# A decoder layer with routed experts on one core: routing, shared expert and experts joined into one stage

## The reference

```
x = layernorm(x + self_attention(x))            # 16 heads of 16, rotary
x = layernorm(x + cross_attention(x, ctx_1024)) # one head of 256
x = layernorm(x + ffn(x))

# ffn, over N = 4096 rows of D = 256
shared = silu(x @ sg.T) * (x @ su.T) @ sd.T     # hidden width 704, padded to 768
shared = shared * sigmoid(x @ shared_gate_w.T)
probs = softmax(x @ gate_w.T)                   # 16 experts
rw, sel = top_k(probs, 2);  rw = rw / rw.sum()
g, h = split(x @ w_gate_up[e]);  expert_e = silu(g) * h @ w_down[e]
ffn = sum over the two chosen e of rw_e * expert_e + shared
```

## Time and profile before

| | |
|---|---|
| three runs | 1185.35, 1186.81 (median), 1187.66 us |
| the profiled execution | 1185.7 us, with a span of 1183.9 us inside it |
| TensorE (PE) busy | 874.0 us, 74% |
| VectorE (DVE) busy | 724.5 us, 61% |
| ScalarE (ACT) busy | 435.5 us, 37% |
| GpSimd (POOL) busy | 409.4 us, 35% |
| mean granted TensorE clock | 0.884 of 2.4 GHz |

### The profile page before, as it was taken

How to read it: one execution, slowest core, us unless ns; L and a number is a source line. 1 busy time by engine, 2 the same in 40 slices (tenths; PEclk the granted TensorE clock), 3 DMA queues, 4 the chain that set the end, 5 groups by cost and what they waited for, 6 DMA issues and landing times. The chain is left out here.

```text
span 1183.9 us, 20916 instructions
## 1 busy us (share of the span) xinstructions
PE 874.0 (74%) x6264; PEld 706.6 (60%) x6265; DVE 724.5 (61%) x1546; ACT 435.5 (37%) x968; POOL 409.4 (35%) x500
## 2 busy tenths in 40 slices
PE   3588888888877288888888410999678778789492
PEld 2465555555544277778777300888578668777382
DVE  5467777767773267777777395244255556467575
ACT  2036565656667133333333122222134334321120
POOL 4322323232310133333333172666500000177664
PEclk8679999999999599999999555899888899999797
DMA  1969989998982724444443344333333344234222
GB/s 62 238 154 248 210 240 219 230 223 209 237 202 60 148 47 99 106 101 106 95 103 80 101 132 150 126 126 107 120 116 116 112 127 135 83 103 143 87 86 71
DMA packets 193065, 161.47 MB, mean 136 GB/s; under 512 B 82160, under 2 KB 179056, under 8 KB 189936
## 3 DMA queue, kind: packets, MB, share of 16 engines
q1 hardware_dynamic: 176368, 133.45, 44.4%
q0 software_dynamic: 6144, 16.79, 4.4%
q10 hardware_dynamic: 10496, 10.49, 2.8%
HBM read 80.86 MB, written 75.37 MB: 132 GB/s over the span
## 5 line engine op out<-in xcount | busy, mean ns | idle before, releaser
L543 DVE TENSOR_REDUCE neg_m<-ps_s 128x2 f32<-128x512 f32 x256 | 169.1, 688 | 37.1 <-PE ps_s L303 36.8
L106 PE MATMUL ps_f<-xg,w_sgu 128*128 128x512 f32 x576 | 146.7, 405 | 48.9 <-DMA xg<-x2T_parts 48.0
L437 ACT ACTIVATE probs<-ps_t 128x512 f32<-128x512 f32 x256 | 147.1, 598 | 95.6 <-PE ps_t L309 91.2
L303 PE MATMUL ps_s<-k_stack,q_stack 48*128 48x256 f32 x512 | 119.0, 335 | 52.6 <-DVE neg_m L543 42.4
L106 PEld LDWEIGHTS ps_f<-xg,w_sgu 128*128 128x128 f32 x576 | 108.8, 195 | 74.0 <-DMA xg<-x2T_parts 49.2
L303 PEld LDWEIGHTS ps_s<-k_stack,q_stack 48*128 48x128 f32 x512 | 76.3, 195 | 109.0 <-DVE neg_m L543 57.0
L309 PE MATMUL ps_t<-q_stack,k_stack 49*128 49x256 f32 x512 | 117.2, 328 | 2.7 <-ACT probs L437 2.7
L106 PE MATMUL ps_g<-w_qkv,x_hl 128*128 128x512 f32 (+1 forms) x384 | 90.9, 386 | 18.6 <-DVE w_qkv L469 11.2
L1426 PE MATMUL ps_f<-w_sdn,hid_hl 128*128 128x256 f32 x576 | 81.8, 294 | 28.3 <-DVE hid_hl L1547 27.9
L1426 PEld LDWEIGHTS ps_f<-w_sdn,hid_hl 128*128 128x128 f32 x576 | 77.5, 198 | 36.5 <-DVE hid_hl L1547 32.3
L106 PE MATMUL ps_f<-w_gu,hid_hl 128*128 x474 | 85.6, 322 | 2.3 <-issue 1.7
(11 more groups left out here) (182 smaller groups left out, 1771.5 us busy)
## 6 DMA issues: line engine op xcount, KB each, us to landing
stacks<-q_hl SPq DMA_DIRECT2D x48, 256.0 KB, 2.8
stacks<-k_hl SPq DMA_DIRECT2D x48, 256.0 KB, 3.5
q_stack<-stacks SPq DMA_DIRECT2D x32, 384.0 KB, 5.8
k_stack<-stacks SPq DMA_DIRECT2D x32, 384.0 KB, 9.2
expert_rows<-no_rows ACTq DMA_DIRECT2D x16, 640.0 KB, 5.5
rows<-expert_rows SPq DMA_DIRECT2D x79, 128.0 KB, 2.1
expert_outputs<-rows SPq DMA_DIRECT2D x79, 128.0 KB, 1.7
heads_out<-o_sb SPq DMA_DIRECT2D x32, 256.0 KB, 9.8
```

Source lines behind the costliest of these rows:

```text
L106: last = pe.matmul(out, lhs(l, c), rhs(r, c), start=(n == 0), stop=(n == len(todo) - 1))
L303: by_query = pe.matmul(ps_s[n % 2][:, k * N:(k + 1) * N], q[q_rows, slab, k * P:(k + 1) * P], kk[q_rows, slab, :], start=True, stop=True)
L437: act.activation(probs[:, n % RING], ps_t[n % 2].rearrange("p (t q) -> p t q", t=TT), ACT.Exp).then_inc(exp_done, 1)
L543: dve.tensor_reduce(neg_m[c][:, :, row], ps_s[n % 2].rearrange("p (t k) -> p t k", t=TT), AX.X, ALU.max, negate=True).then_inc(max_done, 1)
```

## The change

- `routing` and `feed_forward` become one stage, `back_end`. The shared expert starts at once; its first 30 chunks (`EARLY` = 5 groups) run before the experts, 18 after.
- The shared expert's weights are loaded and split in `self_attention`, one piece of 512 columns in each of nine steps: loaded by SP, copied by ACT, subtracted by POOL.
- The routing chain of DVE is cut into pieces that stand between the chunks 0 to 8. PE's two products stand before chunk 4 and use the banks of that chunk.
- The experts' weights are split between the chunks 10 to 21, two pieces of 512 columns in each, by ACT and DVE. POOL splits nothing there.
- POOL's two copies for a tile are gone: the indirect transfers read `pos` and the tile where they lie. As `outputs` overwrites the tile, it waits for the tile's scatter; for the first two groups the result is held in a buffer (`hold`) and added later (`add_held`).
- `BY` is 16, and the check of the loaded values' bounds is left out.
- After the experts the gathered rows have 32 buffers (the dead `w_gu`) in place of 4. POOL takes the root for two tiles at once, and DVE combines two tiles at once; it does 13 of the 16 pairs between the 18 chunks. All of this is written out without loops.

```diff
@@ self_attention, SP, at the end of step(i)
+                j = i.n - S_FIRST
+                if 0 <= j < S_PIECES:
+                    if j >= 2:
+                        sp.wait_ge(s_lo, j - 1)
+                    raw = s_raw[j % 2][:]
+                    sp.dma_start(raw if j < GU_PIECES else raw.rearrange("p (f n) -> p f n", f=2), shared_source(j)
+                                 ).then_inc(s_in[j % 2], 16)
@@ self_attention, ACT, in step(i); POOL subtracts the same piece at the end of its step
+                    if n == 2 and 0 <= i.n - S_FIRST - 1 < S_PIECES:
+                        j = i.n - S_FIRST - 1
+                        act.wait_ge(s_in[j % 2], 16 * (j // 2 + 1))
+                        act.copy(shared_part(0, j), s_raw[j % 2][:]).then_inc(s_hi, 1)
@@ back_end, PE
-            pair(0)
-            with pe.Fori(0, 1) as j:
-                pair(j + 1)
+            chunks(0, FIRST_LATE)
...
-                    block_expert[0:1, bass.ds(BY * turn + c0, c1 - c0)], engines=[mybir.EngineType.PE], min_val=0, max_val=E - 1)
+                    block_expert[0:1, bass.ds(BY * turn + c0, c1 - c0)], engines=[mybir.EngineType.PE], min_val=0, max_val=E - 1,
+                    skip_runtime_bounds_check_because="routing clamps the ids to 0 .. E - 1 on the chip")
@@ back_end, DVE
+            for c in range(FIRST_LATE):
+                gated(c)
+                if c >= SPLIT_AT:
+                    lo(2 * (c - SPLIT_AT))
+                hidden_lo(c)
+                if c >= SPLIT_AT:
+                    lo(2 * (c - SPLIT_AT) + 1)
+                if c == 0:
+                    best()
...
+                if c == 8:
+                    places()
+                if c == 14:
+                    add_held(0)
+                if c == 17:
+                    add_held(1)
+            outputs(EARLY - 1)
...
+            for c in range(FIRST_LATE, CHUNKS):
+                gated(c)
+                hidden_lo(c)
+                if c > FIRST_LATE and c % FC == 0:
+                    outputs(c // FC - 1)
+                if 4 * (c - FIRST_LATE) >= 5 * m + 8 and 2 * m + 2 <= GT * (c // FC):
+                    combine(m)
+                    if m:
+                        norm(m - 1)
+                    m += 1
@@ back_end, POOL
-                pool.tensor_copy(where[c][:], pos[:, :, bass.ds(t, 1)].rearrange("p k o -> p (k o)")).then_inc(where_set, 1)
-                pool.tensor_copy(moved[c][:, 0], tile(t)).then_inc(row_copied, 1)
+            pool.wait_ge(placed, 1)
+            for t in range(TILES):
+                if t >= RING4:
+                    pool.wait_ge(rows_moved[t % RING4], sent(t - RING4))
                 for k in range(2):
-                    pool.indirect_dma_start(out=xs, out_offset=bass.IndirectOffsetOnAxis(ap=where[c][:, k:k + 1], axis=0),
-                                            in_=moved[c][:, 0], in_offset=None).then_inc(scattered[c], 16)
+                    pool.indirect_dma_start(out=xs, out_offset=bass.IndirectOffsetOnAxis(ap=pos[:, k, t:t + 1], axis=0),
+                                            in_=tile(t), in_offset=None).then_inc(rows_moved[t % RING4], 16)
...
+            for m in range(PAIRS):
+                gather(m)
+                if m >= 3:
+                    root(m - 3)
```

More of the change, by code:

```diff
@@ L158, in self_attention @@
         no_rows = sb("no_rows", [D])
+        s_raw = [sb(f"s_raw{p}", [512]) for p in range(2)]
         def psum(name):
@@ L1058, in routing @@
         gate_exp = sb("gate_exp", [TILES])
[L1059 to L1069, removed]
@@ L1111, in _ @@
-        @block.scalar
-        def _(act):
-            act.activation(gate_exp[:], logits[:, :, E], ACT.Exp, scale=-1.0).then_inc(exps_done, 1)
-            for n in range(len(pieces)):
-                act.wait_ge(raw_in[n % RAWS], 16 * (n // RAWS + 1))
-                act.copy(pieces[n][1](0), view(n)).then_inc(raw_hi, 1)
-                if n == 3:
-                    act.wait_ge(gap_ready, 1)
-                    act.activation(gap_exp[:], gap[:], ACT.Exp).then_inc(exps_done, 1)
-        @block.gpsimd
@@ new lines, in rows_sent, with hold, add_held @@
+            def rows_sent(g):
+                for t in range(GT * g, GT * (g + 1)):
+                    dve.wait_ge(rows_moved[t % RING4], sent(t))
+            def hold(g):
+                dve.wait_ge(y_full, g + 1)
+                for q in range(GT):
+                    dve.tensor_scalar(held[g][:, q, :], ps_y[q][:, 0:D], w_shared[:, GT * g + q:GT * g + q + 1], None,
+                                      ALU.mult).then_inc(y_read, 1)
+            def add_held(g):
+                rows_sent(g)
+                dve.wait_ge(y_read, GT * (g + 1))
+                for q in range(GT):
+                    t = GT * g + q
+                    dve.tensor_tensor(tile(t), tile(t), held[g][:, q, :], ALU.add).then_inc(held_added, 1)
@@ new lines, in outputs, with lo @@
+            def outputs(g):
+                dve.wait_ge(y_full, g + 1)
+                rows_sent(g)
+                for q in range(GT):
+                    t = GT * g + q
+                    dve.scalar_tensor_tensor(out=tile(t), in0=ps_y[q][:, 0:D], scalar=w_shared[:, t:t + 1], in1=tile(t),
+                                             op0=ALU.mult, op1=ALU.add).then_inc(y_read, 1)
+            def lo(n):
+                if n < PIECES:
+                    dve.wait_ge(raw_hi, n + 1)
+                    dve.tensor_tensor(piece(1, n), rows[n % RING4][:], piece(0, n).bitcast(F32), ALU.subtract).then_inc(raw_lo, 1)
@@ L1690, in layer @@
+            for m in range(PAIRS - 3, PAIRS):
+                root(m)
 def layer(nc, a, out):
```

696 lines of the change are left out of this document (358 added, 338 removed).

## The result

The changed kernel takes 1146.2 us (median of four runs, 1145.6 to 1151.6), before 1186.8 us: 0.962 of the time, 95% interval 0.957 to 0.966. It is faster, as forecast, but 48 us above the predicted 1098 and outside the range.

What follows compares the result with a forecast made beforehand. The prediction took four stages to be bound by four different things and costed them apart: 1183.9 + 5 - 29 - 28 - 36 = 1096 us of span, so 1098 us of time, range 1072 to 1132.

Steps and rivals of the forecast that it cites:

- PE's own path is the later one by 6 us: Attention to experts: PE's path takes 156 us, POOL's scatter path 150, so PE's sets the stage.
- chunks at 4.21 us: Attention to experts, PE's path: 30 shared-expert chunks at 4.21 us each, 126.3 us.
- 64 x 1.28 = 82: Attention to experts, POOL's path: 64 scatter issues 1.28 us apart last 82 us.
- The front was to be 156: From attention's end to the first experts' block: 185 becomes 156 us, lowest 148, highest 175.
- The slower rival: Scatter beside chunks 10 to 21: DVE holds up POOL's issues, about 1230 us in all; chance 0.03.
- the clock stays low: Shared chunks: at clock 0.73 a chunk takes 5.8 us, 48 more ahead of the experts, 1143 us; chance 0.10.
- Self-attention, +5: Self-attention: nine steps each get a weight piece's transfer, copy and subtraction, +5 us; lowest 0, highest 12.
- Routing between the chunks: DVE's routing chain between chunks costs 25 us, 13 more on PE's path; 128x32 instructions return to 0.2 us.
- the 62 to 70 that were forecast: Sign in the profile: the first indirect scatter issue comes 62 to 70 us after attention's end.
- The experts, 144: Experts' stage: 172 becomes 144 us, with four turn heads of 6.0 us; by the ends, 129 and 158.
- PE passes six products with their six weight loads in 0.95 us: Experts' heads: 0.08 us each, so 14 checks at most 1.1 us and a loaded value at least 0.19.
- After the experts, 120: Last stage: 156 becomes 120 us, from DVE's path 117 and POOL's 116, plus 3; lowest 112, highest 132.

Runs made afterwards that it cites:

- the second train: Changed kernel plus 48 further scatter issues to a spare buffer beside the experts' loop; 1205.0 us, ratio 1.010.
- f1_both_breaks: Changed kernel plus a small POOL power instruction after every fourth scatter issue and after gather issues 4, 8 and 12; 1077.3 us, ratio 0.904.

## Why the prediction was wrong

**The step that failed: "PE's own path is the later one by 6 us".** It rests on two paths costed beside each other: chunks at 4.21 us, and a scatter of "64 x 1.28 = 82". Both numbers are right alone. The scatter took 81 us, and the chunks have 4.21 wherever no train runs. But the one costs the other, and this cost was put at nothing: 80.5 us for three chunks. PE was through its 30 chunks 213.1 us after attention, and with the train broken up after 149.3, so the train cost PE 64 us. The front was to be 156; with the train broken up it is 159.7. That is the whole of the miss: 216.0 - 159.7 = 56 of the 60 us in this stage, against 48 in all.

That 159.7 lies near 156 is partly luck. PE's own path is 149.3 and then the 2.9 us that PE takes to the experts where it waits for no rows, 152 in all: 4 us shorter than summed. The scatter with its breaks is the later path, with 96 us in place of 82.

The trace of before could not price it, since no three indirect issues stand in a row there: a tile's two are followed by POOL's copies. It could have warned: the change took POOL's copies away and counted only their time as gain. An unseen pattern (64 issues without a break in place of pairs) was priced by the rate inside a pair, with no upper end for what it does to others. The range had no case for it.

**The slower rival** had the place right, POOL's issues beside the chunks 10 to 21, and the mechanism turned round: it asked whether DVE would stretch the issues, priced at about 1230 us. The longest issue was 1.46 us; it was the issues that stopped DVE. The Trainium skill's SBUF — State Buffer (SBUF: two separate sides) has the two engines lock each other out of a shared port. That is not what happened: PE and ACT stood still as well, and DVE had no instruction at work from 779 to 822 us.

**The rival "the clock stays low"** gave 1143 us (its own terms, 1098 + 48, give 1146), and the time is 1146, by accident. From 681.5 to 752 us the granted clock was 0.92; it fell to 0.50 only when PE had nothing to do. With the breaks it is 0.98 beside the scatter.

**Self-attention, +5:** +11.0 in this trace, +6.4 on the mean over the thirteen traces that have this stage (-2.4 to +11.4), all against the one trace of before. Most steps still take 20.44 us. Three take 23.2 to 23.6, where before one took 22.7 and two 21.7; one of the three has a wait of PE for ACT's exponential of 2.02 us, in a step with a piece. At 356 us PE is 3.3 us behind the kernel before. Most of the rest comes by 405 us, where the granted clock is lower for nearly the same work. After, then before:

```profile
340.00:400.00 60.00, 48.63 (x390) 27.11 (x386) 23.46 (x36) 35.28 (x69) 0.00 (x0) 0.65 0.40 101
```

```profile
340.00:400.00 60.00, 34.84 (x368) 19.18 (x360) 20.14 (x32) 33.64 (x67) 0.00 (x0) 0.81 0.46 112
```

Whether the pieces bring the lower clock about was not tried.

**Routing between the chunks: right.** The instruction of 128x32 that took 3.13 us beside a POOL split takes 0.195, and the first scatter issue comes 59 us after attention's end, 3 us ahead of the 62 to 70 that were forecast.

**The experts, 144:** 128.4. The mechanism was right, the size of a head too large. Of the two unknown prices the load is the small one: 0.07 us a value, where I took 0.19, above the true value though I called it a lower bound: "PE passes six products with their six weight loads in 0.95 us" says nothing of a check, which took 0.14 and not at most 0.08. And a stall of 2 us costs only 0.6 us of slow clock behind it (pitch of heads 24.9 = 16 x 1.40 + 1.9 + 0.6), where one of 4.17 cost 1.9. The Trainium skill's Runtime: NRT & Kernel Launch (Instruction fetch mechanics) has some 200 ns for a register load; the traces here have about 70 in bulk, and that decides.

**After the experts, 120:** 117.9, for partly the wrong reason. The two waits of DVE, 14 us, were not in the sum; DVE's own work and POOL's path had that much to spare: with the gather's train broken up too the stage is 113.7 us, only 4 shorter.

## What to carry to other kernels

Removing work from an engine that issues indirect transfers also removes the pauses between them; before taking them away, look how many issues have ever stood in a row in a trace, and price a longer row as unknown. When several engines stand still together with nothing to wait for and the transfer engines are not full, look for the one engine that did not stop. Here a pause of 0.94 us in place of 0.30 after every fourth issue was worth 56 us in the stage; 1.53 us per issue on the mean were enough, and 1.45 nearly.

## What the runs showed of the hardware

- Indirect issues by POOL at 1.26 to 1.30 us each, 128 rows of 1 KB, hold up PE, ACT and DVE after some 11 us, and let them go some 5 us after the last. At 1.53 us with even pauses they do not, and at 1.45 they still cost PE 11 us of its path. In the standstill products on PE start up to 2.80 us apart, and an instruction starts up to 16 us after the end of what it waits for (ACT's SiLU ended at 811.0, DVE's product that waits for it started at 827.3), while POOL goes on.
- Scatters and gathers both do it, and it reaches engines in a loop as well as in code written out.
- What it is that fills up stays open. It is not the transfers: the engines were 29% busy and moved 104 GB/s, and each issue's packets had moved 1.1 us after its end. The Trainium skill's Runtime: NRT & Kernel Launch (Instruction fetch mechanics) has instructions come over a queue of transfers of their own. The traces speak against that as the cause: no packet of the "instruction" queues moved while PE's twelve products came one by one (779 to 806 us), nor from 928 to 990 us beside the second train. Whether a request for instructions was held back can't be seen.
- The path of the signals, or of their records, is the rival that is left, and it is untested. Each of the 64 transfers sends 16 signals, 1024 in all; the trace of before has the records of 1015 of them, the changed kernel's of 152, the one with short instructions 150, the one with a break after every eighth 190, after every sixth 251, `f1_both_breaks` 429, and the one with pauses by waiting 728. All executions carry the records from which span and clock are read, so these runs don't tell whether recording takes part in the standstill or only loses records by it.
- A loaded register with its check of bounds costs PE about 0.07 + 2 x 0.14 us; the checks are four fifths of it.
